# Layer norms' statistics in a graph network: one instruction for two interleaved rows, and no aggregation

## What is computed

```python
def _layernorm(x, axis=-1, eps=1e-05):
    m = jnp.mean(x, axis=axis, keepdims=True)
    v = jnp.var(x, axis=axis, keepdims=True)
    return (x - m) / jnp.sqrt(v + eps)

x = _layernorm(x + L0(x, ...))     # two graph convolutions
x = _layernorm(x + L1(x, ...))     # gated convolution, a layer norm inside
x = _layernorm(x + L2(x, ...))     # attention, a layer norm inside
x = _layernorm(x + L3(x, ...))     # six graph convolutions and a dense layer
```

## Time and profile before

| | us |
|---|---|
| median of 3 runs | 10397.67 (10397.62 to 10410.78) |
| profiled execution, its span | 10386.0 |
| DVE busy | 7994.5 (77%) |
| POOL busy | 7618.2 (73%) |
| ACT busy | 5901.6 (57%) |
| PE busy | 6444.3 (62%) |

### The profile page before, as it was taken

One profiled execution on the slowest core, in us unless ns is written; L12 is line 12 of the kernel. 1 busy time (PEld: TensorE's weight loads), 2 busy tenths in 40 slices (PEclk: granted clock), 3 DMA queues, 4 the chain that ended last, 5 costly groups with the idle time before them and its releaser, 6 DMA issues. The chain is left out here.

```text
span 10386.0 us, 141901 instructions
## 1 busy us (share of the span) xinstructions
PE 6444.3 (62%) x32436; PEld 5271.6 (51%) x32436; DVE 7994.5 (77%) x33105; ACT 5901.6 (57%) x13869; POOL 7618.2 (73%) x7194
## 2 busy tenths in 40 slices
PE   6027766667775666677764666687447676664444
PEld 3026655655654666667764666676224444432222
DVE  8359899966666999989988888765558887885554
ACT  0026577767776999979975777633115443433222
POOL 7756688867776888856645777577777777777777
PEclk8569988878886555578876888766558765765555
DMA  3999888842223777734433555465336543442222
GB/s 112 332 298 316 292 283 289 290 141 75 75 74 93 240 235 234 228 120 143 142 121 110 176 175 175 149 178 148 95 93 181 165 115 103 143 123 68 66 68 61
DMA packets 1019498, 1694.44 MB, mean 163 GB/s; under 512 B 304878, under 2 KB 535081, under 8 KB 1018595
## 3 DMA queue, kind: packets, MB, share of 16 engines
q1 hardware_dynamic: 782752, 1361.06, 39.2%
q0 software_dynamic: 175936, 218.82, 9.3%
q10 hardware_dynamic: 59970, 105.49, 2.9%
HBM read 988.03 MB, written 707.78 MB: 163 GB/s over the span
## 5 line engine op out<-in xcount | busy, mean ns | idle before, releaser
L1353 POOL DMA_INDIRECT g_got<-scaled,row_src x2352 | 2228.3, 947 | 794.8 <-issue 661.3
L903 DVE SCALAR_TENSOR_TENSOR g_sums<-g_got,first,g_sums 128x128 f32<-128x128 f32 (+3 forms) x3136 | 868.6, 277 | 1024.0 <-DMA g_got<-scaled,row_src 1013.3
L299 PE MATMUL g_a_p_z<-sb_L_gnn_W,g_a_u_t 128*128 128x128 f32 (+3 forms) x2574 | 611.1, 377 | 564.5 <-ACT g_a_u_t L1186 174.7
L907 DVE SCALAR_TENSOR_TENSOR g_sums<-g_sums,cont,g_got 128x128 f32<-128x128 f32 (+3 forms) x3128 | 880.0, 281 | 0.0
L1186 ACT COPY g_a_u_t<-g_a_p_t 128x512 f32<-128x512 f32 (+3 forms) x495 | 224.9, 454 | 1130.7 <-PE g_a_p_t L1138 599.5
L299 PEld LDWEIGHTS g_a_p_z<-sb_L_gnn_W,g_a_u_t 128*128 128x128 f32 (+1 forms) x2574 | 449.6, 249 | 733.0 <-ACT g_a_u_t L1186 398.7
L299 PE MATMUL g_bb_p_z<-sb_L_gnn_W,g_bb_u_t 128*128 128x128 f32 (+2 forms) x4302 | 762.9, 339 | 69.0 <-DVE g_bb_z L1078 61.3
L299 PEld LDWEIGHTS g_bb_p_z<-sb_L_gnn_W,g_bb_u_t 128*128 128x128 f32 x4302 | 683.1, 239 | 121.9 <-issue 95.6
L1186 ACT COPY g_bb_u_t<-g_bb_p_t 128x1024 f32<-128x1024 f32 (+2 forms) x294 | 233.6, 794 | 806.1 <-PE g_bb_p_t L290 803.5
L2477 POOL DMA_INDIRECT gb_got<-x,row_src x392 | 403.3, 1029 | 242.0 <-POOLq L178 138.0
L458 POOL DMA_INDIRECT f_got<-in_x,idx_dst x396 | 455.8, 1151 | 138.3 <-issue 120.1
(11 more groups left out here) (496 smaller groups left out, 23679.8 us busy)
## 6 DMA issues: line engine op xcount, KB each, us to landing
raw<-gb_u SPq DMA_DIRECT2D x98, 768.0 KB, 3.9
xs<-f_o ACTq DMA_DIRECT2D x97, 516.0 KB
f_x<-in_x ACTq DMA_DIRECT2D x97, 512.0 KB
g_bb_own<-in_x SPq DMA_DIRECT2D x97, 512.0 KB
wide<-g_bb_o SPq DMA_DIRECT2D x97, 512.0 KB
g_bb_own<-wide SPq DMA_DIRECT2D x97, 512.0 KB
g_bb_res<-in_x SPq DMA_DIRECT2D x97, 512.0 KB, 6.7
x<-g_bb_o SPq DMA_DIRECT2D x97, 512.0 KB
```

The lines of the kernel that those rows point to most:

```text
L299: last = nc.tensor.matmul(dst_psum[0:p, q * g * width:(q * g + n) * width], turned_tile[0:n * k, q * P:q * P + p], weight[0:n * k, 0:n * w ...
L903: nc.vector.scalar_tensor_tensor(out=self.firsts, in0=new, scalar=first[:, col], in1=self.firsts, op0=ALU.mult, op1=ALU.add).then_inc(run_ ...
L907: nc.vector.scalar_tensor_tensor(out=self.part(b.s, c), in0=before, scalar=cont[:, col], in1=new, op0=ALU.mult, op1=ALU.add).then_inc(run_ ...
L1353: pool.indirect_dma_start(got[b.s4][:, c * row:(c + 1) * row], None, table, bass.IndirectOffsetOnAxis(ap=index[:, b.n * CH + c:b.n * CH + ...
```

## The change

One BATCH_NORM_STATS2 reads two rows of a partition as one stream of 256 elements, element by element in turn (first of the one, first of the other, second of the one, ...). Its even elements are then the one row and its odd elements the other, and the 6 numbers it writes are count, mean and sum of squared deviations of each row. `root` reads every third number and divides by 128 in the activation's scale; `factors` reads the means where they stand. The aggregation instructions, the tile `mv` and the wait between the two kinds go. In `cn_` the whole `stats` tile is filled with ones at the start in place of `mv`. The same is done in `Norm` (g2, `ga_`, `gb_`, g5 to g8) and `BothNorms` (`cn_`).

```diff
+        def two_rows_each(stats, first, v, p, j):
+
+            for q in range(0, j, 2):
+                last = nc.vector.bn_stats(stats[0:p, 3 * (first + q):3 * (first + q + 2)],
+                                          v[0:p, q * D:(q + 2) * D].rearrange("p (r f) -> p f r", r=2))
+            return last
...
-            def variance(self, link, v, b, ready):
+            def variance(self, v, b, ready):
                 p, j = self.r.pj(b)
-                stats, mv = self.stats[b.s], self.mv[b.s]
-                for q in range(j):
-                    last = nc.vector.bn_stats(stats[0:p, q * 6:q * 6 + 6], v[0:p, q * D:(q + 1) * D])
-                last.then_inc(link.sem, 1)
-                nc.vector.wait_ge(link.sem, link.count())
-                for q in range(j):
-                    last = nc.vector.bn_aggr(mv[0:p, q * 2:q * 2 + 2], stats[0:p, q * 6:q * 6 + 6])
-                last.then_inc(ready, 1)
+                two_rows_each(self.stats[b.s], 0, v, p, j).then_inc(ready, 1)
 
             def root(self, b, ready, guard=eps):
                 p, j = self.r.pj(b)
-                nc.scalar.activation(self.sd[b.s][0:p, 0:j], self.mv[b.s][0:p, 1:2 * j:2], ACT.Sqrt,
-                                     bias=guard[0:p, :]).then_inc(ready, 1)
+                nc.scalar.activation(self.sd[b.s][0:p, 0:j], self.stats[b.s][0:p, 2:3 * j:3], ACT.Sqrt,
+                                     bias=guard[0:p, :], scale=1.0 / D).then_inc(ready, 1)
 
             def factors(self, link, b, ready, minus=None):
 
                 p, j = self.r.pj(b)
-                mv, rstd, nmr = self.mv[b.s], self.rstd[b.s][0:p, 0:j], self.nmr[b.s][0:p, 0:j]
+                means = self.stats[b.s][0:p, 1:3 * j:3]
+                rstd, nmr = self.rstd[b.s][0:p, 0:j], self.nmr[b.s][0:p, 0:j]
...
-                    nc.vector.scalar_tensor_tensor(out=nmr, in0=mv[0:p, 0:2 * j:2], scalar=-1.0, in1=rstd, op0=ALU.mult,
+                    nc.vector.scalar_tensor_tensor(out=nmr, in0=means, scalar=-1.0, in1=rstd, op0=ALU.mult,
                                                    op1=ALU.mult).then_inc(ready, 1)
...
                 def variance(self, b, tiles):
-                    stats, mv = self.stats[b.s], self.mv[b.s]
-                    self.steps.at(b)
                     for (first, p, j), tile in zip(self.rows(b), tiles):
-                        for q in range(j):
-                            last = nc.vector.bn_stats(stats[0:p, 6 * (first + q):6 * (first + q + 1)],
-                                                      tile[0:p, q * D:(q + 1) * D])
-                    last.then_inc(self.steps.sem, 1)
-                    nc.vector.wait_ge(self.steps.sem, self.steps.count())
-                    for first, p, j in self.rows(b):
-                        for q in range(first, first + j):
-                            last = nc.vector.bn_aggr(mv[0:p, 2 * q:2 * q + 2], stats[0:p, 6 * q:6 * q + 6])
+                        last = two_rows_each(self.stats[b.s], first, tile, p, j)
                     last.then_inc(self.varied, 1)
```

More of the change, by code:

```diff
@@ L311, in __init__ @@
                 self.r, n = r, r.per
-                self.stats = [sb(f"{name}_stats{s}", [P, n * 6]) for s in range(2)]
-                self.mv = [sb(f"{name}_mv{s}", [P, n * 2]) for s in range(2)]
+                assert n % 2 == 0
+                self.stats = [sb(f"{name}_stats{s}", [P, n * 3]) for s in range(2)]
                 self.sd = [sb(f"{name}_sd{s}", [P, n]) for s in range(2)]
@@ L1095, in variance @@
                 m = self.m_
-                if not self.deep:
-                    self.link.at(b)
                 nc.vector.wait_ge(m.summed_b if self.deep else m.rows_ready, b.n + 1)
-                self.norm.variance(self.link, self.norm_in[b.n % len(self.norm_in)], b, m.varied)
+                self.norm.variance(self.norm_in[b.n % len(self.norm_in)], b, m.varied)
             def factors(self, b):
@@ L1715, in gated_node_pass, with __init__ @@
                 G = rows_a.per + rows_b.per
-                def __init__(self, sb, name, room, steps, factor_step, varied, rooted, factored, guard):
+                def __init__(self, sb, name, room, factor_step, varied, rooted, factored, guard):
                     G = self.G
-                    self.stats = [sb(f"{name}_stats{s}", [P, 6 * G]) for s in range(2)]
-                    self.mv = [sb(f"{name}_mv{s}", [P, 2 * G]) for s in range(2)]
+                    self.stats = [sb(f"{name}_stats{s}", [P, 3 * G]) for s in range(2)]
                     self.minus = [room(G) for _ in range(2)]
@@ L1723, in __init__ @@
                                                     for n in ("sd", "rstd", "nmr"))
-                    self.steps, self.factor_step = Steps(steps, 1), Steps(factor_step, 1)
+                    self.factor_step = Steps(factor_step, 1)
                     self.varied, self.rooted, self.factored, self.guard = varied, rooted, factored, guard
@@ L1749, in root @@
                     nc.scalar.wait_ge(self.varied, b.n + 1)
-                    nc.scalar.activation(self.sd[b.s][:, :], self.mv[b.s][:, 1:2 * self.G:2], ACT.Sqrt,
-                                         bias=self.guard[:, :]).then_inc(self.rooted, 1)
+                    nc.scalar.activation(self.sd[b.s][:, :], self.stats[b.s][:, 2:3 * self.G:3], ACT.Sqrt,
+                                         bias=self.guard[:, :], scale=1.0 / D).then_inc(self.rooted, 1)
                 def factors(self, b):
@@ L1755, in factors @@
                     nc.vector.wait_ge(self.rooted, b.n + 1)
-                    nc.vector.tensor_scalar(self.minus[b.s], self.mv[b.s][:, 0:2 * self.G:2], -1.0, None, ALU.mult)
+                    nc.vector.tensor_scalar(self.minus[b.s], self.stats[b.s][:, 1:3 * self.G:3], -1.0, None, ALU.mult)
                     nc.vector.reciprocal(self.rstd[b.s][:, :], self.sd[b.s][:, :]).then_inc(self.factor_step.sem, 1)
@@ L1950, in gated_node_pass @@
                 m, o = mark_a, mark_b
-                n1 = BothNorms(sb, "n1", room, m.link, m.factor_step, m.varied, m.rooted, m.factored, eps)
-                n2 = BothNorms(sb, "n2", room, o.link, o.factor_step, m.varied_b, m.rooted_b, m.factored_b, eps_4)
+                n1 = BothNorms(sb, "n1", room, m.factor_step, m.varied, m.rooted, m.factored, eps)
+                n2 = BothNorms(sb, "n2", room, o.factor_step, m.varied_b, m.rooted_b, m.factored_b, eps_4)
                 na = GatedNode(sb, ps, rows_a, beta, p_sc, (n1, n2), mark_b)
@@ L1977, in _ @@
                             for s in range(2):
-                                nc.vector.memset(n.mv[s][:, :], 1.0)
+                                nc.vector.memset(n.stats[s][:, :], 1.0)
                         nc.vector.memset(eps_4[:, :], EPS / 4)
@@ L2069, in stats_1 @@
             def stats_1(self, b):
-                if not self.a:
-                    self.link.at(b)
                 nc.vector.wait_ge(self.m.rows_ready, b.n + 1)
-                self.n1.variance(self.link, self.r_s[b.s], b, self.m.varied)
+                self.n1.variance(self.r_s[b.s], b, self.m.varied)
             def factors_1(self, b):
```

8 lines of the change are left out of this document (4 added, 4 removed).

## The result

| | before | after |
|---|---|---|
| median, us | 10397.65 (10380.44 to 10410.78) | 10125.14 (10120.30 to 10128.34) |
| span of the profiled execution, us | 10386.0 | 10120.5 |

The medians are of four runs each. The ratio is 0.9742 (95% interval 0.973 to 0.9754): 272.5 us faster, 265.5 between the two profiled spans (the span lay 11.7 us under the median before and lies 4.6 under it now). Of the rivals it is nearest to "interleaving is free", and it goes beyond it.

A forecast was written before the change was run, and what follows sets the result against it. DVE was taken to set the step in g2 and ga_, DVE and ACT in cn_, a loop in gb_, POOL in g5 to g8. Savings 30 + 10 + 18 + 17 = 75 us gave 10323 us, range 10185 to 10470.

The forecast's parts named there:

- interleaving is free: Rival for the statistics read: t = 0.328 us, the contiguous pace, saving 223 us in sum, 10175 us; chance 0.18.
- t: Time of one statistics instruction over 256 interleaved elements on DVE: taken as 0.514 us, bounded by 0.328 and 0.593.
- g2: Pass where DVE sets the step: 0.31 us saved in each of 98 steps, 30 us, within POOL's 7.7% of room.
- cn_: Pass where DVE and ACT are both full: ACT's room caps the gain at 10 us, though DVE alone would save 36.
- ga_: Pass where DVE sets the step: one group's saving is lost to nmr waiting for POOL's addition, the other gives 18 us.
- gb_: Pass held by a loop: variance 2's saving becomes a longer wait for the gb_a_x_r load, variance 1 gives 17 us.
- g5 to g8: Passes where POOL's gathers set the step: no gain, since DVE's saving lies under them.
- a step lost at every element: Rival for the statistics read: t = 0.593 us, 99 us slower in sum, 10497 us; chance 0.24.
- Given back: Rival in g2 and ga_: instructions shorten but something hidden behind DVE holds the step; 10371 us; chance 0.06.

The follow-up runs named there:

- e2: The changed kernel with each pair of rows read in 16-byte steps (every fourth element) instead of in turn; 10323.58 us, ratio to before 0.9935.
- e3: The changed kernel with statistics taken of only the first four elements of each row; 10063.61 us, ratio to before 0.9683.
- e4: The kernel before without the aggregations and the wait before them, each row keeping its own statistics instruction of 128 elements; 10144.08 us, ratio to before 0.9761.
- e5: The changed kernel with the copy of the a rows' turned block in cn_ moved from ACT to DVE; 10071.10 us, ratio to before 0.9685.
- e6: The changed kernel with minus the mean put into PSUM in ga_'s two norms, so nmr reads one SBUF tile; 10124.94 us, ratio to before 0.9738.
- e8: The changed kernel with the load of gb_a_x_r issued ahead of the store of raw in SP's gb_ queue; 10058.77 us, ratio to before 0.9676.

## Why the prediction was wrong, step by step

**The step that failed is t**, "if alternating rows pay the same ... t = 0.514 us". Measured: 0.33, the lower bound. The price of the earlier trace rows was right for what it is, a new 16-byte piece at every element: e2 put that read into the kernel, t came out at 0.52, and the time at the forecast's 10323 (to 1 us by luck, as said there). What was wrong is that two rows in turn are such a read. The argument that decided it stood in the rivals ("the two lines in play are each read four times in a row of eight accesses") and got 0.18, since a row of the trace spoke against it. That row shared with the change that accesses are scattered, and not what makes scattered accesses dear. At t = 0.33 the prediction's own rival gives 223 us; the four passes gave 260, and the 37 more lie in `cn_` and `ga_`, where ACT's room was larger than read (below).

**g2**: mechanism and size right at the measured t. DVE would have saved 0.53 + 0.88 = 1.41 us a step, 138 us; POOL let 62 through (69 in the rival). e3 and e4, with a shorter and a longer group, gain the same, so it is no longer DVE; that it is POOL is read from the 647 of 650, and no run made POOL faster.

**`cn_`**: that ACT caps the pass was right (e5), but its room was mis-sized, 10 us against 29.5. "991.4 of 1000" counts each instruction to its recorded end, and the end overlaps the next start when the queue is full. The timeline of ACT in `cn_` of the kernel before has both cases in one step:

```profile
3700.48 0.31 ACT L1750 ACTIVATE cn_n_sd<-cn_n_mv,cn_eps 128x12 f32<-128x12 f32 x1
...
3705.50 0.29 ACT L1750 ACTIVATE cn_n_sd<-cn_n_mv,eps 128x12 f32<-128x12 f32 x1
3705.69 1.63 ACT L1764 ACTIVATE cn_a_o<-cn_a_y,cn_n_nmr,cn_n_rstd 128x128 f32<-128x128 f32 x4
...
3710.77 1.00 ACT L1914 COPY cn_b_x_t<-cn_b_p_x 128x1024 f32<-128x1024 f32 x1
3711.79 0.30 ACT L1750 ACTIVATE cn_n_sd<-cn_n_mv,cn_eps 128x12 f32<-128x12 f32 x1
```

The root at 3705.50 is recorded with 0.29 us, and the next instruction starts 0.19 behind it. The other root is followed only after 0.39 us (its successor starts at 3700.87), and the copy of 1024 after 1.02. The same view of the kernel after:

```profile
3700.32 0.53 ACT L1739 ACTIVATE cn_n_sd<-cn_n_stats,eps 128x12 f32<-128x12 f32 x1
...
3705.59 1.25 ACT L1903 COPY cn_b_x_t<-cn_b_p_x 128x1024 f32<-128x1024 f32 x1
3706.50 0.55 ACT L1739 ACTIVATE cn_n_sd<-cn_n_stats,cn_eps 128x12 f32<-128x12 f32 x1
3706.71 1.88 ACT L1753 ACTIVATE cn_a_y<-cn_a_v,cn_n_nmr,cn_n_rstd 128x128 f32<-128x128 f32 x4
...
3711.33 0.54 ACT L1739 ACTIVATE cn_n_sd<-cn_n_stats,eps 128x12 f32<-128x12 f32 x1
```

Now both roots are followed after 0.20 and 0.21, the copy after 0.91, though the records have become longer (0.53 instead of 0.29). The step went from 11.31 (3700.48 to 3711.79) to 11.01 us (3700.32 to 3711.33): 99 x 0.30 = 30 us. It could have been read before the change: the root's part in the same step, the copy's in `ga_`, where a copy of 1024 is followed after 0.89 us (4903.37 to 4904.26). The Trainium skill, Perfetto Trace Analysis, section Optimizing Scalar/DVE Operations, says of Scalar and DVE that the write-acknowledgement half of an instruction's profiled latency overlaps with the next instruction; the root's 0.29 beside 0.19 agrees.

**`ga_`**: "the addition starts when add_x has ended, so it doesn't move against the group" failed. Timeline of DVE and POOL after:

```profile
4801.56 1.23 DVE L2084 TENSOR_TENSOR ga_b_y<-ga_b_y,ga_b_x_beta 128x1024 f32<-128x1024 f32 x1
4802.36 2.64 POOL L2121 TENSOR_TENSOR ga_b_x_beta<-ga_b_x,row_L_gnn_ln_b 128x1024 f32<-128x1024 f32 x1
4802.82 1.42 DVE L310 BATCH_NORM_STATS2 ga_b_n_stats<-ga_b_y 128x6 f32<-128x256 f32 x4
...
4804.38 0.65 DVE L346 SCALAR_TENSOR_TENSOR ga_b_n_nmr<-ga_b_n_stats,ga_b_n_rstd 128x8 f32<-128x8 f32 x1
```

The addition now starts while add_x still runs, 0.46 us ahead of the group; before it came 0.11 us behind the group's start, with POOL idle 2.21 us for add_x. That wait is gone (by count, the addition works two blocks ahead of add_x now and four before, so the buffer that it waited for has long been free), and the meeting that the prediction named does happen: `nmr` takes 0.65 us instead of 0.17 and ends with the addition (4802.36 + 2.64 = 4805.00). But it costs nothing (e6), since ACT is the limit. The same root of ACT before, in a stretch in which each of its instructions starts ahead of the recorded end of the last, and after:

```profile
4899.90 0.30 ACT L331 ACTIVATE ga_b_n_sd<-ga_b_n_mv,eps 128x8 f32<-128x8 f32 x1
...
4908.24 0.31 ACT L331 ACTIVATE ga_b_n_sd<-ga_b_n_mv,eps 128x8 f32<-128x8 f32 x1
```

```profile
4799.35 0.60 ACT L331 ACTIVATE ga_b_n_sd<-ga_b_n_stats,eps 128x8 f32<-128x8 f32 x1
...
4807.70 0.61 ACT L331 ACTIVATE ga_b_n_sd<-ga_b_n_stats,eps 128x8 f32<-128x8 f32 x1
```

So ACT's own work took 8.34 us a step before, while the step was 9.42 (add_x from start to start), and now the step is that work, 8.35 to 8.36. It could have been read before the change. About 1.06 us a step came out, where the rival had 0.93 for one group alone and took the other for lost. By the count used in g2 POOL looks full here, too: 591.88 and 81.1 of "issue" make 673 of 680.

```profile
POOL att_e L2191 <- issue: 81.1, 288, 0.3
```

But one gather a step and the addition are recorded longer beside DVE's gain and add_x (1.78 and 2.64 us instead of 0.94 and 2.35); without that it would need some 7.2 of the 8.36 us, an estimate from these numbers. No run took work off ACT or POOL in this pass. In e2 the 18 us that the prediction gave came out as 19.6, but not for its reason: `nmr` took 39.0 us in all 196 instructions of the pass, against 39.8 before, so it met the addition no more than before, and both groups shrank by some 0.1 us each.

**`gb_`**: that one group's saving counts and the other's is lost was right (0.53 x 99 = 53 against 56), also in e2 (16 against 17). The form was not. What DVE waited for in front of the second instruction of `rows`, over the whole pass (us, times), before and after:

```profile
  DMA gb_a_x_r<-x: 66.5, 94
```

```profile
  DMA gb_a_x_r<-x: 77.7, 91
```

The wait grew by 11 us, 0.11 a step, not by 0.53. More of the rest is `nmr`, which in norm 2 meets POOL's addition in this pass now. The busy time of all 198 `nmr` on DVE, before and after:

```profile
5300.00:6700.00 1400.00, 37.84 (x198) 0.79 0.45 152
```

```profile
5300.00:6700.00 1400.00, 67.52 (x198) 0.77 0.53 172
```

That is 30 us more, 0.30 a step. It lies between the load's issue and its use as well, so it costs no more than the wait would have; the load sets the step, as e8 shows.

**g5 to g8**: forecast 0, measured 5.6 + 1.7 = 7 us in all, 0.3% of these passes; the cause stays open. **The other rivals**: a step lost at every element is out by t. Given back did not happen: the steps of g2 and `ga_` are held by POOL and ACT, and not by a new wait behind DVE.

## What to carry to other kernels

Before a price is taken over from a row that looks alike, ask what in it is paid for, and whether the new instruction does that too: here 16-byte steps touch a new 16-byte piece with each element and return to it, if at all, 64 elements later, while two rows in turn are back in the same piece at every second element, and that was free. Where an engine's room caps a gain, count it from start to start of instructions that are back to back, not from the busy share, which also counts recorded ends under which the next instruction could already run. When a gain has used up an engine's lead, the next one lies with the engine that is full then: moving one copy and one load's issue gave another 151 us.

## What the runs showed of the hardware

- DVE reads two rows in turn at the contiguous pace: an addition over rows 2352 bytes apart (1395 against 1382 ns for 1176 elements) and statistics over rows 512 bytes apart (0.34 against 0.33 us for 256). Four rows in turn or more cost about as much as 16-byte steps (2151 and 2397 against 2236 ns; 0.48 to 0.49 against 0.50 us). Three rows were not tried, nor a third distance between two rows.
- In `ga_` POOL's addition starts 0.80 us after add_x's start both after the change and in e6, right behind a gather that is recorded with 1.78 us instead of 0.94. By count no semaphore of add_x holds the addition there; that the gather takes longer beside gain and add_x is seen in the trace, and why is not shown.
